# Latent attention: side steps interleaved by the engine that empties their bank, values in front of the scores, scale moved into q

## The chip, the cores and the metric

One NeuronCore of a Trainium2 chip runs the whole program. The metric is the device time of one execution in microseconds (us). TensorE is called PE in the profile, VectorE DVE, ScalarE ACT, GpSimd POOL, SyncE SP.

## What is computed

A decoder with two layers, of which this change touches one part, the cross attention of layer 1 (called latent attention here). For each of 16 batches, 100 latent rows (the running x) attend to 361 context rows and to themselves, with 16 heads of 64:

```python
xn = layer_norm(x, g_x, b_x)          # context, 361 x 256
ln = layer_norm(latents, g_l, b_l)    # 100 x 256
q = ln @ Wq                           # 256 x 1024
k, v = split(concat([xn, ln], axis=1) @ Wkv)   # 461 rows
q = q * 64 ** -0.5
sim = where(full_mask, einsum('bhid,bhjd->bhij', q, k), max_neg)
out = einsum('bhij,bhjd->bhid', softmax(sim), v) @ Wout
return layer_norm(out, g_o, b_o)      # added to x, normed again
```

## The kernel before

The program is a row of stages, one after the other, with a barrier between them: self attention, cross attention, an expert adapter, bucket attention, latent attention (`latent_attention`, tiles named `la_`), and a routed feed-forward. Only latent attention is touched. All of it is in float32 apart from the mask.

The 16 heads of a batch are handled in 8 pairs. Each engine has its own instruction queue, written out by hand, and the queues meet in counting semaphores. A batch has 8 slots (m = 0 to 7), one for each pair of heads. In slot m the queues do this:

- PE: `scores(m)` (2 mask matmuls in bfloat16 and 4 of 461 columns, into one of two pairs of PSUM banks), `turn` of the pair before (8 transposes of the probabilities), `values` of the pair before that (16 matmuls), and up to three side steps.
- DVE: `norm` of the pair before (one reciprocal, two multiplications), `maxima(m)` (one reduction over both heads, then the multiplication by minus the scale), in slots 3 to 7 some of the layer norms (`out_norm` in 3, `x_norm` in 4, `inputs` for the batch after next in 5, `apply_inputs` in 6, `mask` in 7), and then its part of the side steps.
- ACT: the first side step if it is ACT's, `exps(m)` (two Exp with their sums), the second, `evac` (copies the turned probabilities out of PSUM), `sums` (copies the values' result), the third.

The side steps prepare the next batch, and end the one before. They are named in `SLOTS`: `fl` and `fc0`, `fc1` turn the inputs, `fk0` to `fk7` project keys, `fq0`, `fq1` queries, `fv00` to `fv31` values, and `by` is the output projection of the batch before. All of them write one PSUM bank, `pf` (in the profile `la_side`): a step waits until the step before it has been read out (`above(pe, s_R, n)`). ACT reads `fl`, `fc` and `fk` out, DVE reads `fq`, `fv` and `by`. Each queue runs through the steps in the order of `SLOTS`. Before the first batch, the run-in does the steps of batch 0 alone, one after the other, and the last batch (15) has no side step but `by`.

PE's order in a slot is: scores, side step 1, turn, side step 2, values, side step 3.

Of the kernel before, what the change touches and what calls it, by code (L numbers as in the profile page):

```python
# [10 lines left out]
ALU = mybir.AluOpType  # L11
ACT = mybir.ActivationFunctionType
AX = mybir.AxisListType.X

P = 128
NB, T, D = 16, 100, 256
# [28 lines left out]
class Stage:  # L45
# [15 lines left out]
    def sb(self, name, shape, dt=F32):  # L61
        return self.ctx.enter_context(self.nc.sbuf_tensor(f"{self.name}_{name}", shape, dt))

    def ps(self, name, shape):
        return self.ctx.enter_context(self.nc.psum_tensor(f"{self.name}_{name}", shape, F32))

    def sem(self, name):
        self.sems.append(self.nc.alloc_semaphore(f"{self.name}_{name}"))
        return self.sems[-1]
# [13 lines left out]
class Side:  # L83
# [11 lines left out]
    def steps(self, i, m):  # L95

        first, last = isinstance(i, int) and i == 0, isinstance(i, int) and i == NB - 1
        keep = [s for s in self.all if not (first and s[0] == "b") and not (last and s[0] == "f")]
        if first:
            base = len(self.fronts)  # L100
        else:
            base = 2 * len(self.fronts) + (i - 1) * len(self.all)
        return [(s, base + keep.index(s)) for s in self.slots[m] if s in keep]

    def prologue(self):
        return [(s, n) for n, s in enumerate(self.fronts)]
# [661 lines left out]
def cross_attention(nc, X, ident, d):  # L768
# [4 lines left out]
    keys = [P, P, SC - 2 * P]  # L773
    SLOTS = [["fx"], ["fc0", "fq"], ["fc1", "bo"], ["bp", "fv0"], ["fk0", "by"], ["fk1", "fv1"], [], []]
    NORM = 6
    st = Stage(nc, "ca")
    with st:
# [35 lines left out]
        s_dv = sem("dve_chain")  # L813
        side = Side(SLOTS, s_F, s_R)
        NW = 5
# [612 lines left out]
def bucket_attention(nc, X, ident, d):  # L1428
# [3 lines left out]
    SCALE = D ** -0.5  # L1432
    SLOTS = [["fx", "fq"], ["fh"], [], ["fv", "bo"]]
    st = Stage(nc, "ba")
    with st:
# [33 lines left out]
        s_dv, s_dq, s_df, s_pl = sem("setup_chain"), sem("quad_chain"), sem("step_chain"), sem("pool_chain")  # L1469
        side = Side(SLOTS, s_F, s_R)  # L1470
        NW = 5 + HG
# [299 lines left out]
def latent_attention(nc, X, ident, d):  # L1771
# [3 lines left out]
    NC, SK = 4, SC + T  # L1775
    KP_ = NC * P
    MP = NH // 2
    SCALE = DX ** -0.5
    ckeys = [P, P, SC - 2 * P]
    keys = [min(P, SK - c * P) for c in range(NC)]  # L1780
    SLOTS = [["fl", "fc0", "fc1"], ["fk0", "fk1", "fk2"], ["by", "fk3", "fk4"], ["fk5", "fk6", "fk7"],
             ["fq0", "fq1", "fv00"], ["fv01", "fv10", "fv11"], ["fv20", "fv21", "fv30"], ["fv31"]]
    st = Stage(nc, "la")
    with st:
        sb, ps, sem = st.sb, st.ps, st.sem
# [11 lines left out]
        qT = [sb(f"qT{b}", [P, NE, T]) for b in range(2)]  # L1797
        nm = [sb(f"nm{b}", [T, 2]) for b in range(2)]
# [8 lines left out]
        pS = ps("pS", [P, 4, 512])  # L1807
        pPT = ps("pPT", [P, 2, 512])
        pav, pf = ps("pav", [P, 4, T]), ps("side", [P, 512])
# [3 lines left out]
        s_xs, s_F, s_R = sem("xs_staged"), sem("side_filled"), sem("side_read")  # L1813
        s_cmv, s_cln, s_crs, s_n = (sem(n) for n in ("input_stats", "input_log", "input_rstd", "inputs_normed"))
        s_mb = sem("mask_ready")
        s_S, s_mx, s_P, s_Z = sem("scores_in_psum"), sem("max_ready"), sem("exp_ready"), sem("probs_ready")
# [3 lines left out]
        s_dv, s_dn, s_dy, s_dz = sem("setup_chain"), sem("input_chain"), sem("out_chain"), sem("norm_chain")  # L1820
        side = Side(SLOTS, s_F, s_R)
        NW = 10

        with nc.Block() as block:
# [25 lines left out]
            def _(pe):  # L1850
# [36 lines left out]

                def scores(i, b, m):
                    n = i * MP + m
                    if m == 0:  # L1890
                        pe.wait_ge(s_R, side.front_done(i))
                        pe.wait_ge(s_mb, i + 1)
                    above(pe, s_P, n - 1)
                    half = [slice(DX * e, DX * (e + 1)) for e in range(2)]
                    o = [pS[0:T, 2 * (m % 2) + e, 0:SK] for e in range(2)]
                    for e in range(2):
                        nc.tensor.matmul(o[e], row0[half[e], 0:T], mb[b][half[e], 0:SK], start=True, stop=False)
                    for e in range(2):
                        last = nc.tensor.matmul(o[e], qT[b][half[e], m, :], kT[b][half[e], m, :],  # L1899
                                                start=False, stop=True)  # L1900
                    last.then_inc(s_S, 1)
# [7 lines left out]
                                                       pr[m % 2][:, e, c * P:(c + 1) * P], ident[0:T, 0:T])  # L1909
                    last.then_inc(s_PTp, 1)  # L1910

                def values(n, b, m):
                    pe.wait_ge(s_PT, n + 1)
                    above(pe, s_av, n)
                    for c in range(NC):
                        for e in range(2):
                            last = nc.tensor.matmul(pav[DX * e:DX * (e + 1), m % 4, :],  # L1917
                                                    v[b][:, c, (2 * m + e) * DX:(2 * m + e + 1) * DX],
                                                    pT[m % 2][:, e, c * T:(c + 1) * T], start=c == 0, stop=c == NC - 1)
                    last.then_inc(s_AV, 1)  # L1920

                def body(i, b):

                    first = isinstance(i, int) and i == 0
                    for m in range(MP):
                        n = i * MP + m
                        small = side.steps(i, m) + [None] * 3

                        def between(s):
                            if s and s[0] == "by":  # L1930
                                pe.wait_ge(s_av, i * MP)
                                step(*s, i - 1, b)
                            elif s:
                                step(*s, i + 1, 1 - b)
                        scores(i, b, m)
                        between(small[0])
                        if m >= 1 or not first:
                            turn(n - 1, (m - 1) % MP)
                        between(small[1])
                        if m >= 2:  # L1940
                            values(n - 2, b, m - 2)
                        elif not first:
                            values(n - 2, 1 - b, MP - 2 + m)
                        between(small[2])

                pe.wait_ge(s_w, 16 * NW)
# [3 lines left out]
                over_batches(pe, body)  # L1950
                n = NB * MP
                turn(n - 1, MP - 1)
                values(n - 2, 1, MP - 2)
                values(n - 1, 1, MP - 1)
                pe.wait_ge(s_av, n)
                for name, k in side.epilogue():
                    step(name, k, NB - 1, 0)
# [2 lines left out]
            def _(dv):  # L1960
# [35 lines left out]
                def step(name, n, i, b):  # L1996
                    if name[:2] == "fq":
                        dv.wait_ge(s_F, n + 1)
                        nc.vector.tensor_copy(qT[b][:, 4 * int(name[2]):4 * int(name[2]) + 4, :],
                                              pf[:, 0:4 * T].rearrange("p (q t) -> p q t", q=4)).then_inc(s_R, 1)  # L2000
                    elif name[:2] == "fv":
                        c, h = int(name[2]), int(name[3])
                        dv.wait_ge(s_F, n + 1)
                        nc.vector.tensor_copy(v[b][0:keys[c], c, h * 512:(h + 1) * 512], pf[0:keys[c], :])\  # L2004
                            .then_inc(s_R, 1)
                    elif name == "by":
                        dv.wait_ge(s_F, n + 1)
                        nc.vector.tensor_copy(y0[:], pf[0:T, 0:D]).then_inc(s_R, 1)
                        dv.wait_ge(s_R, n + 1)
                        link(nc.vector.bn_stats(stats[:], y0[:]), i, 1)  # L2010
                        nc.vector.memset(gap[:], 0.0)
                        nc.vector.bn_aggr(mv[:], stats[:]).then_inc(s_mv, 1)
# [21 lines left out]
                def maxima(i, m):  # L2034
                    n = i * MP + m
                    dv.wait_ge(s_S, n + 1)
                    above(dv, s_P, n - 1)
                    nc.vector.reduce_max(nm[m % 2][:], pS[0:T, 2 * (m % 2):2 * (m % 2) + 2, 0:SK], AX)\  # L2038
                        .then_inc(s_mx, 1)
                    dv.wait_ge(s_mx, 2 * n + 1)  # L2040
                    nc.vector.tensor_scalar(nm[m % 2][:], nm[m % 2][:], -SCALE, None, ALU.mult).then_inc(s_mx, 1)  # L2041

                def norm(n, m):
                    dv.wait_ge(s_P, n + 1)
# [57 lines left out]
            def _(ac):  # L2102
# [29 lines left out]

                def exps(i, m):
                    n = i * MP + m
                    ac.wait_ge(s_mx, 2 * n + 2)
                    above(ac, s_PTp, n - 1)
                    for e in range(2):
                        ins = nc.scalar.activation(pr[m % 2][:, e, 0:SK], pS[0:T, 2 * (m % 2) + e, 0:SK], ACT.Exp,  # L2138
                                                   bias=nm[m % 2][:, e:e + 1], scale=SCALE,
                                                   accum_out=zs[m % 2][:, e:e + 1])  # L2140
                    ins.then_inc(s_P, 1)

# [45 lines left out]
                n = NB * MP  # L2188
# [458 lines left out]
```

## Time and profile before

| | us |
|---|---|
| median of 3 runs | 3083.02 |
| lowest, highest | 3065.78, 3084.93 |
| profiled execution, its own time | 3084.47 |
| its span in the profile | 3082.7 |
| run-in of latent attention, batches 0 to 14, batch 15 up to its last turn | 60.51, 955.05, 33.88 |

The time of the profiled execution is the span and 1.8 us around it. A clock of 1.00 in the rows is 2.4 GHz, the other level, 0.50, is 1.2 GHz; a mean between them tells the share of the time at each. Of a PE row in a timeline, the start is the first matmul's, and several matmuls of one step are merged with their count behind the x. The last row of the table is cut from the trace at the first matmuls of the scores of batch 0 (1789.06 us) and of batch 15 (2744.11 us).

### The profile page before, as it was taken

Reading aid. Unit: us, or ns where it says so; the run is one execution under the profiler, and the core shown is the slowest. Engines: PE = TensorE matmul, PEld = TensorE weight load, DVE = VectorE, ACT = ScalarE, POOL = GpSimd, SP = SyncE. Lnnn points to the kernel's source line nnn. Section 1 sums busy time; section 2 is a strip of 40 time slices with the busy share of each in tenths; the row PEclk is TensorE's granted clock in tenths of the full one; section 3 lists DMA queues with packets and bytes.
Section 4 is the critical chain, followed back from the end, with each engine's and each line's share of the span. In section 5 each row is a group of like instructions: output and inputs, shape, how many; then the busy total and the mean of one; then the engine's idle time right before and its main releaser. Section 6 shows DMA issues by size and latency. Waiting matters only on the chain. (4 is left out here: it accounts for less than half of the span.)

```text
span 3082.7 us, 44584 instructions
## 1 busy us (share of the span) xinstructions
PE 2467.7 (80%) x15278; PEld 1459.9 (47%) x15279; DVE 1723.8 (56%) x3404; ACT 1187.7 (39%) x2418; POOL 433.1 (14%) x360
## 2 busy tenths in 40 slices
PE   3777777774999999876777489999999999994793
PEld 1333333332666666553444145554455544553572
DVE  3899999993555555534777234444544454453123
ACT  1666666663333333222444124343343433440110
POOL 1333333220111111002343000000000000001102
PEclk9888888885999999977787699999999999995897
DMA  3000000000000000200000200000000000006111
GB/s 110 1 1 0 0 0 0 0 0 27 13 13 10 14 10 10 68 4 9 0 0 0 72 5 11 5 5 5 5 10 5 5 5 5 5 1 229 40 32 51
DMA packets 50289, 60.41 MB, mean 20 GB/s; under 512 B 9764, under 2 KB 44889, under 8 KB 49770
## 3 DMA queue, kind: packets, MB, share of 16 engines
q1 hardware_dynamic: 47218, 53.69, 5.5%
q0 software_dynamic: 3008, 5.91, 0.7%
q8 instruction: 36, 0.59, 0.1%
q14 instruction: 27, 0.22, 0.0%
HBM read 51.06 MB, written 8.52 MB: 19 GB/s over the span
## 5 line engine op out<-in xcount | busy, mean ns | idle before, releaser
L1880 PE MATMUL la_side<-la_wkv,la_inT 128*128 128x512 f32 (+1 forms) x512 | 258.0, 627 | 49.2 <-DVE la_v L2004 48.3
L2138 ACT ACTIVATE la_pr<-la_pS,la_nm 100x461 f32<-100x461 f32 x256 | 163.1, 644 | 267.9 <-DVE la_nm L2041 267.9
L1868 PE MATMUL la_side<-la_inT,la_wkv 128*128 128x461 f32 x512 | 240.1, 592 | 7.6 <-ACT la_kT L2125 6.9
L2038 DVE TENSOR_REDUCE la_nm<-la_pS 100x2 f32<-100x922 f32 x128 | 142.7, 1115 | 182.9 <-PE la_pS L1899 182.9
L300 PE MATMUL sa_pS<-sa_qT,sa_kTm 128*100 128x400 f32 x512 | 195.1, 504 | 7.3 <-DVE sa_L L471 7.3
L2004 DVE COPY la_v<-la_side 128x512 f32<-128x512 f32 (+1 forms) x128 | 87.7, 685 | 180.1 <-PE la_side L1880 180.0
L895 PE MATMUL ca_pS<-ca_kT,ca_qTm 128*100 128x361 f32 x512 | 187.0, 488 | 0.5 <-DVE ca_va L974 0.5
L1075 ACT ACTIVATE ca_pr<-ca_pS,ca_nm 100x361 f32<-100x361 f32 x256 | 129.7, 559 | 125.2 <-DVE ca_nm L1009 125.1
L1006 DVE TENSOR_REDUCE ca_nm<-ca_pS 100x2 f32<-100x722 f32 x128 | 116.3, 908 | 96.6 <-PE ca_pS L895 96.5
L604 ACT ACTIVATE sa_L<-sa_L 100x800 f32<-100x800 f32 x128 | 111.3, 870 | 146.8 <-DVE sa_L L471 146.8
L1880 PEld LDWEIGHTS la_side<-la_wkv,la_inT 128*128 128x128 f32 (+1 forms) x512 | 82.3, 180 | 163.6 <-DVE la_v L2004 91.5
L2206 POOL TENSOR_TENSOR la_xb<-io_X,la_bo 100x256 f32<-100x256 f32 x16 | 11.6, 727 | 958.4 <-DVE io_X L2031 958.4
L2125 ACT COPY la_kT<-la_side 128x461 f32<-128x461 f32 x128 | 69.5, 543 | 198.8 <-PE la_side L1868 198.8
L1868 PEld LDWEIGHTS la_side<-la_inT,la_wkv 128*128 128x128 f32 x512 | 89.3, 194 | 101.9 <-issue 54.8
L479 DVE TENSOR_TENSOR sa_L<-sa_L,sa_sm 100x3200 f32<-100x3200 f32 x32 | 122.4, 3824 | 19.8 <-ACT sa_L L611 19.8
L470 DVE TENSOR_TENSOR sa_sm<-sa_pS,sa_causal 100x800 f32<-100x800 f32 x128 | 125.9, 984 | 5.4 <-PE sa_pS L300 5.3
L1908 PEld LDWEIGHTS la_pPT<-io_ident,la_pr 100*128 100x128 f32 x1024 | 100.9, 142 | 52.5 <-issue 38.2
L1917 PEld LDWEIGHTS la_pav<-la_pT,la_v 128*64 128x64 f32 x2048 | 93.6, 139 | 62.7 <-issue 56.9
L1899 PE MATMUL la_pS<-la_kT,la_qT 64*100 64x461 f32 x512 | 120.8, 550 | 0.0
L1917 PE MATMUL la_pav<-la_pT,la_v 128*64 128x100 f32 x2048 | 118.7, 259 | 0.4 <-ACT la_oT L2150 0.4
L1908 PE MATMUL la_pPT<-io_ident,la_pr 100*128 100x100 f32 x1024 | 110.1, 250 | 7.1 <-DVE la_pr L2048 7.1
L916 PE MATMUL ca_pav<-ca_pT,ca_va 128*32 128x100 f32 x1536 | 115.7, 253 | 0.0
(385 smaller groups left out, 4924.1 us busy)
## 6 DMA issues: line engine op xcount, KB each, us to landing
rf_w<-in_L_ffn_W SPq DMA_DIRECT2D x16, 1024.0 KB, 13.3
ca_cn<-in_ctx SPq DMA_DIRECT2D x16, 256.0 KB, 2.7
la_cn<-in_ctx SPq DMA_DIRECT2D x16, 256.0 KB, 2.7
rows_in<-io_zero SPq DMA_DIRECT2D x20, 128.0 KB, 4.6
rb_xr<-rows_in POOLq DMA_DIRECT2D x20, 128.0 KB, 2.2
rows_out<-rb_yr SPq DMA_DIRECT2D x20, 128.0 KB, 1.7
ea_wc<-in_L_ffn_conv_W SPq DMA_DIRECT2D x1, 2048.0 KB
la_wkv<-in_L_xattn_Wkv SPq DMA_DIRECT2D x1, 2048.0 KB
```

The source lines that it names most:

```text
L300: last = nc.tensor.matmul(pS[0:T, 2 * (m % 2) + e, 0:NBR * T], kTm[:, g, h + e, :], qT[:, g, :, :], start=True, stop=True)
L470: cm.after(nc.vector.tensor_tensor(sm[:, g, h:h + 2, :, :], two, mask, ALU.add))
L479: nc.vector.tensor_tensor(L[:, par, g].rearrange("p h r t -> p (h r t)"), L[:, par, g].rearrange("p h r t -> p (h r t)"), sm[:, g].rearran ...
L895: last = nc.tensor.matmul(pS[0:T, 2 * (m % 2) + e, 0:SC], qTm[b][:, h // HG, h % HG, :], kT[b][:, h // HG, :], start=True, stop=True)
L1075: ins = nc.scalar.activation(pr[m % 2][:, e, 0:SC], pS[0:T, 2 * (m % 2) + e, 0:SC], ACT.Exp, bias=nm[m % 2][:, e:e + 1], scale=SCALE)
L1868: last = nc.tensor.matmul(pf[:, 0:SK], wkv[:, k, e * P:(e + 1) * P], inT[:, k, :], start=k == 0, stop=k == KD - 1)
L1880: last = nc.tensor.matmul(pf[0:keys[c], :], inT[:, k, c * P:c * P + keys[c]], wkv[:, k, o:o + 512], start=k == 0, stop=k == KD - 1)
L1899: last = nc.tensor.matmul(o[e], qT[b][half[e], m, :], kT[b][half[e], m, :], start=False, stop=True)
L1908: last = nc.tensor.transpose(pPT[:, e, c * T:(c + 1) * T], pr[m % 2][:, e, c * P:(c + 1) * P], ident[0:T, 0:T])
L1917: last = nc.tensor.matmul(pav[DX * e:DX * (e + 1), m % 4, :], v[b][:, c, (2 * m + e) * DX:(2 * m + e + 1) * DX], pT[m % 2][:, e, c * T:(c ...
L2038: nc.vector.reduce_max(nm[m % 2][:], pS[0:T, 2 * (m % 2):2 * (m % 2) + 2, 0:SK], AX)\
L2138: ins = nc.scalar.activation(pr[m % 2][:, e, 0:SK], pS[0:T, 2 * (m % 2) + e, 0:SK], ACT.Exp, bias=nm[m % 2][:, e:e + 1], scale=SCALE, accu ...
```

## The change

Five edits, all in latent attention:

1. `SLOTS` is written anew, so that most neighbouring side steps are read out by different engines. The same 22 steps are done.
2. PE's order in a slot becomes: values, scores, side step 1, turn, side step 2, side step 3. The values of a pair are still taken two slots after its scores.
3. The scores no longer wait for all side steps of their batch: scores 0 and 4 wait for the keys and queries of the next four pairs, and the first values of a batch wait for the rest.
4. The scale is multiplied into q while q is read out of PSUM (a `tensor_copy` becomes a `tensor_scalar` with one multiplication), and Exp gets no scale.
5. `reduce_max` gives the negated maximum itself (`negate=True`), and the `tensor_scalar` on 100x2 elements behind it (L2041) goes, with its wait and its count of `s_mx`.

```diff
+    def later(self, a, b):
+
+        return max(a, b, key=self.all.index)
...
-    SLOTS = [["fl", "fc0", "fc1"], ["fk0", "fk1", "fk2"], ["by", "fk3", "fk4"], ["fk5", "fk6", "fk7"],
-             ["fq0", "fq1", "fv00"], ["fv01", "fv10", "fv11"], ["fv20", "fv21", "fv30"], ["fv31"]]
+    SLOTS = [["fl", "fc0", "fc1"], ["fk0", "fv00", "fk1"], ["by", "fv01"], ["fk2", "fv10", "fk3"],
+             ["fq0", "fv11", "fk4"], ["fk5", "fv20", "fq1"], ["fk6", "fv21", "fk7"], ["fv30", "fv31"]]
...
                 def scores(i, b, m):
                     n = i * MP + m
+                    if m % 4 == 0:
+                        pe.wait_ge(s_R, side.read_of(i, side.later(f"fk{m + 3}", f"fq{m // 4}")))
                     if m == 0:
-                        pe.wait_ge(s_R, side.front_done(i))
                         pe.wait_ge(s_mb, i + 1)
...
-                def values(n, b, m):
+                def values(n, i, b, m):
+                    if m == 0:
+                        pe.wait_ge(s_R, side.front_done(i))
                     pe.wait_ge(s_PT, n + 1)
...
+                        if m >= 2:
+                            values(n - 2, i, b, m - 2)
+                        elif not first:
+                            values(n - 2, i - 1, 1 - b, MP - 2 + m)
                         scores(i, b, m)
                         between(small[0])
                         if m >= 1 or not first:
                             turn(n - 1, (m - 1) % MP)
                         between(small[1])
-                        if m >= 2:
-                            values(n - 2, b, m - 2)
-                        elif not first:
-                            values(n - 2, 1 - b, MP - 2 + m)
                         between(small[2])
...
-                        nc.vector.tensor_copy(qT[b][:, 4 * int(name[2]):4 * int(name[2]) + 4, :],
-                                              pf[:, 0:4 * T].rearrange("p (q t) -> p q t", q=4)).then_inc(s_R, 1)
+                        nc.vector.tensor_scalar(qT[b][:, 4 * int(name[2]):4 * int(name[2]) + 4, :],
+                                                pf[:, 0:4 * T].rearrange("p (q t) -> p q t", q=4), SCALE, None,
+                                                ALU.mult).then_inc(s_R, 1)
...
-                    nc.vector.reduce_max(nm[m % 2][:], pS[0:T, 2 * (m % 2):2 * (m % 2) + 2, 0:SK], AX)\
+                    nc.vector.reduce_max(nm[m % 2][:], pS[0:T, 2 * (m % 2):2 * (m % 2) + 2, 0:SK], AX, negate=True)\
                         .then_inc(s_mx, 1)
-                    dv.wait_ge(s_mx, 2 * n + 1)
-                    nc.vector.tensor_scalar(nm[m % 2][:], nm[m % 2][:], -SCALE, None, ALU.mult).then_inc(s_mx, 1)
...
-                    ac.wait_ge(s_mx, 2 * n + 2)
+                    ac.wait_ge(s_mx, n + 1)
                     above(ac, s_PTp, n - 1)
                     for e in range(2):
                         ins = nc.scalar.activation(pr[m % 2][:, e, 0:SK], pS[0:T, 2 * (m % 2) + e, 0:SK], ACT.Exp,
-                                                   bias=nm[m % 2][:, e:e + 1], scale=SCALE,
+                                                   bias=nm[m % 2][:, e:e + 1],
                                                    accum_out=zs[m % 2][:, e:e + 1])
```

## Rows read from the trace of the kernel before

**Rows 1.** The page: busy time, share and instructions of each engine
```profile
PE 2467.7 (80%) x15278; PEld 1459.9 (47%) x15279; DVE 1723.8 (56%) x3404; ACT 1187.7 (39%) x2418; POOL 433.1 (14%) x360
```

**Rows 2.** Windows: batches 0 to 14, batch 15; busy time by engine, clock, DMA
```profile
1789.06:2744.11 955.05, 892.45 (x5344) 485.94 (x5344) 453.40 (x1113) 377.18 (x980) 15.00 (x28) 0.99 0.02 6
2744.11:2777.99 33.88, 26.18 (x258) 17.11 (x257) 21.48 (x54) 19.48 (x54) 0.72 (x1) 1.00 0.00 1
```

**Rows 3.** Waits of PE in batches 0 to 14: total us, times, longest
```profile
PE la_side L1880 <- DVE la_v L2004: 42.8, 28, 1.8
```

**Rows 4.** Timeline of POOL, one row per batch: start us, length, instruction, idle before
```profile
2077.24 0.73 POOL L2206 TENSOR_TENSOR la_xb<-io_X,la_bo 100x256 f32<-100x256 f32 x1 [64.18 <-DVE io_X L2031]
...
2142.41 0.73 POOL L2206 TENSOR_TENSOR la_xb<-io_X,la_bo 100x256 f32<-100x256 f32 x1 [64.10 <-DVE io_X L2031]
...
2206.04 0.73 POOL L2206 TENSOR_TENSOR la_xb<-io_X,la_bo 100x256 f32<-100x256 f32 x1 [62.56 <-DVE io_X L2031]
```

**Rows 5.** Timeline of PE in slots 3 to 5 of one batch
```profile
2067.28 1.82 PE L1868 MATMUL la_side<-la_inT,la_wkv 128*128 128x461 f32 x4
2068.93 0.85 PE L1908 MATMUL la_pPT<-io_ident,la_pr 100*128 100x100 f32 x8
2069.73 1.82 PE L1868 MATMUL la_side<-la_inT,la_wkv 128*128 128x461 f32 x4
...
2080.65 1.98 PE L1880 MATMUL la_side<-la_wkv,la_inT 128*128 128x512 f32 x4
2082.57 0.40 PE L1897 MATMUL la_pS<-la_mb,la_row 64*100 64x461 bf16 x2
...
2083.67 1.98 PE L1880 MATMUL la_side<-la_wkv,la_inT 128*128 128x512 f32 x4
...
2088.07 3.46 PE L1880 MATMUL la_side<-la_wkv,la_inT 128*128 128x512 f32 x4 [1.73 <-DVE la_v L2004]
```

**Rows 6.** Timeline of all engines, end of slot 7 and slot 0
```profile
2042.57 0.91 PE L1917 MATMUL la_pav<-la_pT,la_v 128*64 128x100 f32 x16
...
2043.40 0.40 PE L1897 MATMUL la_pS<-la_mb,la_row 64*100 64x461 bf16 x2
...
2044.71 1.12 DVE L2038 TENSOR_REDUCE la_nm<-la_pS 100x2 f32<-100x922 f32 x1 [0.39 <-PE la_pS L1899]
...
2047.48 0.65 ACT L2121 ACTIVATE la_inT<-la_side,la_bx,la_gx 128x361 f32<-128x361 f32 x1
...
2048.02 0.83 ACT L2146 COPY la_pT<-la_pPT 128x800 f32<-128x800 f32 x1
...
2048.19 0.53 PE L1862 MATMUL la_side<-io_ident,la_cn 128*128 128x128 f32 x3 [1.07 <-ACT la_inT L2121]
...
2048.65 0.40 PE L1897 MATMUL la_pS<-la_mb,la_row 64*100 64x461 bf16 x2
```

**Rows 7.** Timeline of the run-in, side steps alone on PE
```profile
1742.06 3.44 PE L1868 MATMUL la_side<-la_inT,la_wkv 128*128 128x461 f32 x4 [0.63 <-ACT la_kT L2125]
...
1767.02 1.99 PE L1880 MATMUL la_side<-la_wkv,la_inT 128*128 128x512 f32 x4 [0.67 <-DVE la_qT L1999]
...
1769.78 1.99 PE L1880 MATMUL la_side<-la_wkv,la_inT 128*128 128x512 f32 x4 [0.78 <-DVE la_v L2004]
```

**Rows 8.** Timeline of all engines, one slot of batch 15
```profile
2770.47 1.11 DVE L2038 TENSOR_REDUCE la_nm<-la_pS 100x2 f32<-100x922 f32 x1
...
2771.62 0.17 DVE L2041 TENSOR_SCALAR la_nm<-la_nm 100x2 f32<-100x2 f32 x1
2771.82 0.65 ACT L2138 ACTIVATE la_pr<-la_pS,la_nm 100x461 f32<-100x461 f32 x1 [1.47 <-DVE la_nm L2041]
...
2773.08 0.82 ACT L2146 COPY la_pT<-la_pPT 128x800 f32<-128x800 f32 x1
...
2773.78 0.26 ACT L2150 COPY la_oT<-la_pav 128x100 f32<-128x100 f32 x1
2774.16 1.11 DVE L2038 TENSOR_REDUCE la_nm<-la_pS 100x2 f32<-100x922 f32 x1
```

More of the change, by code:

```diff
@@ L1952, in _ @@
                 turn(n - 1, MP - 1)
-                values(n - 2, 1, MP - 2)
-                values(n - 1, 1, MP - 1)
+                values(n - 2, NB - 1, 1, MP - 2)
+                values(n - 1, NB - 1, 1, MP - 1)
                 pe.wait_ge(s_av, n)
```

## The prediction

> **What bounds the kernel now.** I read the page first: PE is busy 80% of the span, more than any other engine [rows 1]. That is a mean over six stages, so I cut out the one that changes. In its batches 0 to 14 PE is busy 892.5 of 955.1 us at a granted clock of 0.99, while DVE and ACT are under half busy [rows 2]. The stage is bound by PE's own work, and what can be won is only the idle time between its matmuls (about 62 us) and the time at the low clock: a mean of 0.99 is some 2% of 955 us, 20 us, at half rate, which costs at most 10. Work taken from DVE or ACT gains nothing unless PE waits for it. The waits of PE show where it does: 42.8 us in 28 waits for DVE's copy of the values, two per batch [rows 3]. The timeline puts one of them, 1.73 us, behind `fv01` in slot 5 [rows 5]; the other, of 1.35 us, is in slot 6 (2 x 14 waits of 3.1 us in sum per batch). In both slots DVE does a layer-norm block between the maximum and the copy. A third wait, 1.07 us, is ACT's: `fc1` in slot 0 waits for the copy of `fc0`, which is queued behind `exps(0)` [rows 6]. One batch takes 63.6 us, and 65.2 with a clock drop in it [rows 4]: there the matmuls behind the 1.73 us wait took 3.46 us in place of 1.98 [rows 5].
>
> In batch 15, without side steps, another thing bounds: the cycle maximum, exps, norm, next maximum, 3.69 us per slot (2770.47 to 2774.16) [rows 8], with PE often idle: 26.2 of 33.9 us [rows 2].
>
> **Part 1, the new slots: the old stalls.** With `fv` now second in its slot, the copy has the first step, the turn and the `fv` itself as cover. After the scores DVE needs about 1.3 us to the start of the maximum and 1.1 for it [rows 6], and the longest block of layer norm adds about 2 us (it ends before 4.5 us), while the `fv` ends at about 1.10 + 1.65 + 0.80 + 1.98 = 5.5 us [rows 5]. So DVE is free in time in slots 3 to 6, and both waits go: -3.1 us per batch.
>
> **Part 2, the order: new gaps.** The bank `pf` is still one. Before, each side step had something of PE's own behind it: the turn (0.80), the values (0.83), or the scores (1.10) [rows 5, 6]. The turn covers the copy of an `fk` exactly: `fk6` starts at 2069.73 as the turn ends [rows 5]. Now side steps 2 and 3 are neighbours with nothing between them, and it does not matter which engine empties the bank, since step 3 waits for it. The run-in shows this bare sequence: from one `fv` to the next 2.76 us, with 0.78 us of idle PE [rows 7], against 1.92 us from an `fv` to the scores, where nothing is waited for [rows 5]. The gap costs 0.84 us. Five slots have it (1, 3, 4, 5, 6), always behind an `fv`: +4.2 us per batch. In slot 7 the turn covers all but 0.1 us of `fv30`'s copy; slot 2 has no third step.
>
> **Part 3, slot 0.** It took 5.25 us (2043.40 to 2048.65) [rows 6]. Take the start of its scores as zero. `fc1` starts at 4.79; without L2041 the exps and all behind them come 0.2 us earlier (0.17 us of the instruction [rows 8] and its step): 4.59, and it has issued at 5.05. Then the values come, and no longer the scores. They wait for `evac` of the pair before and, since `values` also waits for the previous `sums`, for that too: `evac` starts at 4.62 - 0.2 = 4.42, `sums` starts 0.70 behind it and takes 0.26 [rows 6, 8], so the values start at 5.43 and the next scores at 6.27. Slot 0 grows by 1.0 us. The values that used to lie between `fc0` and `fc1` were cover, and are now outside.
>
> Per batch: -3.1 + 4.2 + 0.1 + 1.0 = +2.2 us. Fifteen batches have side steps for the next: +33 us. I walked the other slots in the same way: `norm` is always done over 1 us before its turn, except in slot 0 (about 0.2), and `evac` ends before `values` needs it.
>
> **Part 4, batch 15.** ACT's order is exps(m), evac(m-1), sums(m-2). The next maximum now needs the next scores, these are queued behind `values(m-1)` on PE, and these need evac and sums. From the start of the exps: sums end 2.22 us later (2771.82 to 2773.78 + 0.26) [rows 8], values at 2.27, scores at 3.10, maximum 1.31 later [rows 6] at 4.4, next exps 1.15 later at 5.5. The cycle was 3.69 us and is 5.5, though L2041 is gone: +1.8 us for seven cycles, less where `by` already lengthened one: +12 us (bounds: -1.5, if only L2041 counts, to +15).
>
> **Part 5, what is on no path.** In batches 0 to 14 the removed L2041 (128 x 0.17 us in all) lies beside PE's side steps except in slot 0, where it is counted. Nothing in the trace shows a negating reduction; bounds are the plain 1.11 us [rows 8] and that plus the removed 0.17, and I take the plain one. Also q's read-out with a multiplication has no row: its copy is covered by the turn or followed by values and scores, so between -0.1 and +0.5 us per copy come to nothing to a few us; I take 0. Of that the Trainium skill, "VectorE: DVE Perf Modes", section "Why PSUM operands drop a tier", says that float32 from PSUM runs at the plain rate, copy or not; no row here shows the multiplication from PSUM. The two waits that PE's scores and first values now have are for steps a slot or more old. The run-in does the same steps with the same gaps in another order: 0, give or take 3.
>
> **Part 6, the clock.** A drop costs about 1.5 us (65.17 - 63.63) [rows 4] and came behind a 1.73 us wait. These go: -6 us of the 10. But slot 0 now idles 1.7 us before `fc1` and 0.4 behind it, with small steps between: bounds no drop (0) and one in each batch (+22); I take half, +11. In batch 15, PE is busy only some 2.8 of 5.5 us per cycle, where it was 2.8 of 3.7 at the full clock [rows 2, 8]. At half rate values and scores, which are on the new path, take about twice their 1.9 us: bounds 0 and +13; I take +6.
>
> **Sum.** 33 + 12 - 6 + 11 + 6 = +56 us on the profiled execution's own 3084.5: 3140 us, 1.8% slower. That execution is within 2 us of the median of the runs, so this is also the forecast for the median.
>
> **The rivals.** (a) *The gap behind side step 2 is not paid*, because PE finds the bank emptied or loads weights meanwhile. For it: matmul ends are modelled and the weight loads overlap. Against it: the bare sequence in the run-in, eight times over. The time is 3140 - 75 g for a gap smaller by g; with no gap left, 3077, not slower. It decides from a gap below 0.1 us; with the clock undisturbed, below 0.3. Chance 0.10, with 0.05 for over 1% faster, where slot 0 is also shorter than I read. (b) *Only the steady part counts*: batch 15 doesn't lengthen, and the clock stays up. 3084.5 + 33 - 6 = 3111, within 1%. For it: the clock stayed at 1.00 in batch 15. Against it: the order of three queues. Chance 0.10. (c) *The clock falls with each small gap.* Five gaps per batch, each with its next step at 1.2 GHz: 3.44 us for an `fk` as against 1.82 [rows 5, 7], +1.6 x 75 = +122: 3262 us. For it: `fk` steps with 0.63 us gaps between them stayed at that level at 1742 us [rows 7]. Against it: at 1767 and 1769 us steps with gaps of 0.67 and 0.78 us ran at the full 1.99 [rows 7]. The Trainium skill, "TensorE: Matmul & The Clock Gate", section "A second HAM failure mode: psum-queue depth-cycling", says that idle bits between matmul groups that wait for PSUM can make the clock swing. By that rule (c) would happen; the run-in of this trace shows both. Chance 0.05.
>
> **How the numbers follow.** The forecast has 0.75. Some 1% is what a measurement of this kernel can tell from no change, as its runs lie 0.6% apart. Above +1% (3114) are the forecast, but for a small part, and (c): 0.79. Within 1%: (b) and half of (a) and that part: 0.16. Faster: 0.05. The range reaches down past (b), with 15 us for a run on the low side of the spread, to 3098, and up to the upper bounds of the clock terms (11 + 7), rounded to 3165; (c) and (a) stay outside.
>
> **What would show it.** In the profile after: no wait of PE for DVE above 1 us in slots 5 and 6; about 70 waits of 0.8 us, before `fk1`, `fk3`, `fk4`, `fq1`, `fk7`, all for DVE's copy of `la_v`; a batch period near 65.8 us; slot 0 of 6.3 us; exps of batch 15 5.5 us apart, with the scores' releaser before DVE's maximum; L2041 gone and the reduction at 1.1 us. A period below 63.6 us would mean that Part 2 is wrong; an even 3.5 us in batch 15, Part 4.

## The result

The changed kernel takes 3142.0 us (median of 4 runs, 3136.3 to 3145.7), the kernel before 3077.6 us beside it (4 runs, 3065.8 to 3084.9). The ratio is 1.021, with a 95% interval from 1.017 to 1.025: the change makes the kernel 2.1% slower. The profiled execution took 3145.65 us, with a span of 3143.9 us, 61.2 us more than before.

**Where the 61.2 us are.** Cutting both traces at the same four marks (first side step of the stage, first scores of batch 0, first scores of batch 15, last turn) gives:

| stretch, us | before | after | difference |
|---|---|---|---|
| all earlier stages, up to the first side step | 1728.6 | 1722.2 | -6.4 |
| run-in | 60.5 | 59.6 | -0.9 |
| batches 0 to 14 | 955.1 | 1000.5 | +45.5 |
| batch 15, to its last turn | 33.9 | 56.3 | +22.4 |
| rest | 304.7 | 305.3 | +0.6 |

The earlier stages are not touched, and the start of this stage lies between 1713.0 and 1728.6 us in the nine profiles of this study. The whole loss lies in the batches. The windows after, with the columns of [rows 2] (start and end, length, then the busy time of PE, PEld, DVE, ACT and POOL, the clock and the DMA):

```profile
1781.75:2782.29 1000.54, 905.65 (x5363) 489.77 (x5362) 433.95 (x994) 374.85 (x981) 15.13 (x28) 0.98 0.02 5
2782.29:2838.57 56.28, 37.23 (x243) 23.17 (x241) 20.67 (x46) 18.69 (x52) 0.72 (x1) 0.72 0.00 1
```

PE is busy 905.7 us in batches 0 to 14, where it was 892.5, and idle 95 us where it was 63 [rows 2]. In batch 15 the mean clock is 0.72, and it was 1.00. The waits of PE in batches 0 to 14 (total us, times, longest), where [rows 3] had 28 waits for DVE of up to 1.8 us:

```profile
PE la_side L1872 <- DVE la_v L2012: 47.0, 60, 0.8
PE la_side L1866 <- ACT la_inT L2127: 24.5, 15, 1.9
PE la_side L1878 <- DVE la_v L2012: 11.8, 15, 0.8
PE la_pav L1924 <- ACT la_oT L2156: 7.0, 15, 1.2
```

Seventy-five waits for DVE's copy of the values, none above 0.8 us, five in each of the 15 batches. A new releaser stands in the list: the values wait for ACT's `sums` (`la_oT`), 15 times. The wait for the copy of `fc0` has grown from 15.8 to 24.5 us in all. The batch period on POOL's timeline, as in [rows 4]:

```profile
2150.65 0.74 POOL L2212 TENSOR_TENSOR la_xb<-io_X,la_bo 100x256 f32<-100x256 f32 x1 [66.42 <-DVE io_X L2039]
...
2216.59 0.73 POOL L2212 TENSOR_TENSOR la_xb<-io_X,la_bo 100x256 f32<-100x256 f32 x1 [64.86 <-DVE io_X L2039]
...
2284.07 0.74 POOL L2212 TENSOR_TENSOR la_xb<-io_X,la_bo 100x256 f32<-100x256 f32 x1 [66.41 <-DVE io_X L2039]
```

The starts are 65.94 and 67.48 us apart, without and with a clock drop (a stretch at 1.2 GHz). They were 63.63 and 65.17.

The timeline of PE, a slot 0 with a clock drop first, then a gap in slot 3 and one in slot 5; it answers to [rows 5]:

```profile
2051.06 0.53 PE L1866 MATMUL la_side<-io_ident,la_cn 128*128 128x128 f32 x3 [1.70 <-ACT la_inT L2127]
2052.01 1.32 PE L1924 MATMUL la_pav<-la_pT,la_v 128*64 128x100 f32 x16 [0.42 <-ACT la_oT L2156]
2053.26 0.62 PE L1902 MATMUL la_pS<-la_mb,la_row 64*100 64x461 bf16 x2
...
2055.35 2.00 PE L1872 MATMUL la_side<-la_inT,la_wkv 128*128 128x461 f32 x4
...
2074.95 1.98 PE L1884 MATMUL la_side<-la_wkv,la_inT 128*128 128x512 f32 x4
2077.72 1.82 PE L1872 MATMUL la_side<-la_inT,la_wkv 128*128 128x461 f32 x4 [0.78 <-DVE la_v L2012]
...
2095.77 2.03 PE L1878 MATMUL la_side<-la_inT,la_wq 128*128 128x100 f32 x16 [0.79 <-DVE la_v L2012]
```

From the `fv` at 2074.95 to the next side step at 2077.72 it is 2.77 us, as in the run-in before; the row's own idle time is 0.78 us. In slot 0, PE idles 1.70 us in front of `fc1`, does 0.53 us, idles 0.42 us in front of the values, and then the clock is low: the values' 16 matmuls take 1.32 in place of 0.91 us, and the scores 1.74 in place of 0.94.

A slot 0 without a drop, all engines, answers to [rows 6]:

```profile
2181.50 0.40 PE L1902 MATMUL la_pS<-la_mb,la_row 64*100 64x461 bf16 x2
...
2182.81 1.12 DVE L2046 TENSOR_REDUCE la_nm<-la_pS 100x2 f32<-100x922 f32 x1 [0.41 <-PE la_pS L1904]
...
2183.85 0.53 PE L1866 MATMUL la_side<-io_ident,la_cn 128*128 128x128 f32 x3 [0.17 <-ACT la_inT L2121]
2184.12 0.65 ACT L2144 ACTIVATE la_pr<-la_pS,la_nm 100x461 f32<-100x461 f32 x1 [0.33 <-DVE la_nm L2046]
...
2185.38 0.65 ACT L2127 ACTIVATE la_inT<-la_side,la_bx,la_gx 128x361 f32<-128x361 f32 x1
...
2185.92 0.83 ACT L2152 COPY la_pT<-la_pPT 128x800 f32<-128x800 f32 x1
```

From the start of the scores (2181.50), the exps start at 2.62, the copy of `fc0` at 3.88 and `evac` at 4.42 us, each 0.2 us earlier than before, but PE comes to them sooner than that.

One cycle of batch 15, all engines, answers to [rows 8]:

```profile
2821.87 0.65 ACT L2144 ACTIVATE la_pr<-la_pS,la_nm 100x461 f32<-100x461 f32 x1 [4.85 <-DVE la_nm L2046]
...
2823.12 0.82 ACT L2152 COPY la_pT<-la_pPT 128x800 f32<-128x800 f32 x1
...
2823.83 0.26 ACT L2156 COPY la_oT<-la_pav 128x100 f32<-128x100 f32 x1
...
2824.23 1.60 PE L1924 MATMUL la_pav<-la_pT,la_v 128*64 128x100 f32 x16 [2.74 <-ACT la_oT L2156]
...
2825.76 0.62 PE L1902 MATMUL la_pS<-la_mb,la_row 64*100 64x461 bf16 x2
...
2827.66 1.12 DVE L2046 TENSOR_REDUCE la_nm<-la_pS 100x2 f32<-100x922 f32 x1 [3.37 <-PE la_pS L1904]
2828.82 0.65 ACT L2144 ACTIVATE la_pr<-la_pS,la_nm 100x461 f32<-100x461 f32 x1 [4.73 <-DVE la_nm L2046]
```

From exps to exps it is 6.95 us (2821.87 to 2828.82), where it was 3.69. In order: `evac`, `sums`, values behind them at the low clock (1.60 us), scores behind the values, the maximum behind the scores, the exps behind the maximum. The maximum used to start with no idle time of DVE in front of it [rows 8]; now DVE idles 3.37 us until the scores are there.

### The profile page after: what moved, and what is told of

It reads as the page before. It is cut to its first block and busy times, and to the rows that moved or that the text cites. A ratio compares the mean times of both kernels' runs of the same rounds, so it can differ in the third digit from the quotient of the medians.

```text
span 3143.9 us, 44398 instructions
## 1 busy us (share of the span) xinstructions
PE 2475.9 (79%) x15278; PEld 1462.0 (47%) x15279; DVE 1702.9 (54%) x3276; ACT 1184.6 (38%) x2418; POOL 433.6 (14%) x360
## 5 line engine op out<-in xcount | busy, mean ns | idle before, releaser
L1904 PE MATMUL la_pS<-la_kT,la_qT 64*100 64x461 f32 x512 | 132.2, 597 | 0.0
L2152 ACT COPY la_pT<-la_pPT 128x800 f32<-128x800 f32 x128 | 106.1, 829 | 32.0 <-PE la_pPT L1913 29.6
```

## The experiments

Two groups of runs, each beside the kernel before on its chip (median 3078.6 us beside e1 to e4, 3080.2 beside e5 to e7; 7 runs each).

**e1, the old order of PE's queue, all else as changed.**

```diff
-                        if m >= 2:
-                            values(n - 2, i, b, m - 2)
-                        elif not first:
-                            values(n - 2, i - 1, 1 - b, MP - 2 + m)
                         scores(i, b, m)
...
                         between(small[1])
+                        if m >= 2:
+                            values(n - 2, i, b, m - 2)
+                        elif not first:
+                            values(n - 2, i - 1, 1 - b, MP - 2 + m)
                         between(small[2])
```

> The changed kernel with the old order in PE's queue (the values between side step 2 and side step 3), all else as changed. My theory: the five gaps of 0.8 us per batch are covered again, slot 0 falls from 6.3 to about 5.05 us, batch 15 goes back to a cycle of 3.5 us; a batch takes about 60.5 us without a clock drop, and the whole about 3030 us, 1.7% faster than the kernel before. Rival (the new slots themselves cost, since each side step now goes back and forth between two busy engines): the time stays above 3100 us. Rival (mostly the clock): the drops stay at one in nearly each batch.

Measured: 3021.4 us, ratio to before 0.982 (0.980 to 0.984), so some 120 us less than the changed kernel. A batch takes 60.4 us (60.34 and 60.42 in turn), and the two windows are:

```profile
1783.95:2687.39 903.44, 885.29 (x5346) 483.30 (x5346) 432.62 (x994) 384.52 (x980) 15.07 (x28) 1.00 0.02 6
2687.39:2719.84 32.45, 26.16 (x258) 17.10 (x256) 20.11 (x46) 19.00 (x53) 0.72 (x1) 1.00 0.00 1
```

All of the loss is in the order, and the other edits are a gain of 1.8%. PE has no wait for DVE left but one of 0.8 us in all these batches, and the mean clock is 1.00, with one drop, in slot 0 of batch 0. Both rivals fall.

**e2, the kernel before with the new order alone.**

```diff
+                        if m >= 2:
+                            values(n - 2, b, m - 2)
+                        elif not first:
+                            values(n - 2, 1 - b, MP - 2 + m)
                         scores(i, b, m)
...
                         between(small[1])
-                        if m >= 2:
-                            values(n - 2, b, m - 2)
-                        elif not first:
-                            values(n - 2, 1 - b, MP - 2 + m)
                         between(small[2])
```

> The kernel before with the new order in PE's queue alone. My theory: the order is what costs. With the old slots it makes six bare neighbours (fk1 to fk2, fk3 to fk4, fk6 to fk7 at 0.63 us of idle PE; fq1 to fv00, fv10 to fv11, fv21 to fv30 at 0.7 to 0.8), slot 0 grows by 1.2 us and the two old waits for DVE in slots 5 and 6 stay: about +5.7 us per batch, +86 us, and batch 15 grows by 20 us or more; about 3195 us in all, slower than the changed kernel. Rival (the new slots cost): near 3083 us.

Measured: 3200.8 us, ratio 1.040 (1.038 to 1.043). PE's waits in batches 0 to 14:

```profile
PE la_side L1880 <- DVE la_v L2004: 54.5, 58, 1.3
PE la_side L1868 <- ACT la_kT L2125: 27.9, 44, 0.6
PE la_side L1862 <- ACT la_inT L2121: 27.8, 15, 2.1
PE la_pav L1917 <- ACT la_oT L2150: 24.4, 30, 1.6
PE la_side L1880 <- DVE la_qT L1999: 10.0, 15, 0.7
```

The order alone costs 4%, and every kind of gap is there: 44 of 0.63 us behind an `fk`, 15 of 0.67 behind `fq1`, and 58 for the copy of the values: two new ones of 0.78 us per batch, and the two old ones in 14 batches, now about 1.32 and 0.93 us long. The gaps follow from the neighbours in one bank, whichever engine reads it: `fk1` and `fk2`, both read by ACT, pay 0.63 us, and `fq1` and `fv00`, both read by DVE, 0.67. A batch takes 69.8 us, and 71.4 with a clock drop, which nearly each has. That is 6.2 us more than before, where I had expected 5.7: the values of slot 0 also wait for `sums`, 1.12 us in front of the scores, besides the 0.42 us in slot 1 (30 waits in the list). Batch 15 takes 55.1 us in place of 33.9, so the order alone lengthens it.

**e3, the kernel before with the scale in q and the negated maximum alone** (edits 4 and 5 of the diff).

> The kernel before with the scale in q and the negated maximum alone. My theory: 0.2 us per batch in slot 0 and 0.2 us per slot in batch 15, in all 4 to 5 us, 0.15%, which is at the edge of what can be measured; the cycle of batch 15 is 3.5 us as against 3.69. Rival (DVE's small instruction is on the path in every slot): 0.2 us x 128 = 26 us faster, 3057 us.

Measured: 3059.3 us, ratio 0.994 (0.992 to 0.997), 17 us faster by the ratio, and not 5. A batch takes 62.8 us as against 63.5 to 63.6, and the 65.2 of a batch with a drop is not seen. So my expectation missed, and so did its rival (26 us in every slot). Here are DVE and PE in slot 5 of e3, then DVE in slot 5 of the kernel before:

```profile
2002.06 1.11 DVE L2039 TENSOR_REDUCE la_nm<-la_pS 100x2 f32<-100x922 f32 x1
...
2003.09 1.07 DVE L1973 BATCH_NORM_STATS2 la_cst<-la_cn 128x6 f32<-128x256 f32 x3
...
2004.82 0.66 DVE L2005 COPY la_v<-la_side 128x512 f32<-128x512 f32 x1
...
2005.54 0.70 PE L1880 MATMUL la_side<-la_wkv,la_inT 128*128 128x512 f32 x1 [1.35 <-DVE la_v L2005]
```

```profile
2018.97 1.11 DVE L2038 TENSOR_REDUCE la_nm<-la_pS 100x2 f32<-100x922 f32 x1
...
2020.39 1.08 DVE L1973 BATCH_NORM_STATS2 la_cst<-la_cn 128x6 f32<-128x256 f32 x3
...
2022.13 0.66 DVE L2004 COPY la_v<-la_side 128x512 f32<-128x512 f32 x1
```

From the start of the maximum to the start of the first layer-norm instruction it is 1.03 us, and the copy of `fv01` comes 2.76 us after the maximum. In the kernel before these are 1.42 and 3.16 us: the removed instruction of 0.17 us stood in front of the copy that PE waited for. PE's waits for DVE fall from 42.8 to 34.8 us in sum. I had counted L2041 in slot 0 alone. It also lay on the path in slots 5 and 6, as long as those had their waits (here 1.35 and 1.16 us, before 1.73 and 1.35). With 0.4, 0.2 and 0.2 us in slots 5, 6 and 0 (there the wait for `fc0`, 12.8 us in sum in place of 15.8) that is 0.8 us per batch, 12 us. In the profiles batches 0 to 14 shrank by 16.9 us and batch 15 by 1.4; the rest of the 16.9 fits the clock, with one drop in these batches in place of five, but was not measured by itself.

**e4, the changed kernel with the old order in batch 15 alone.** (`take()` holds the four lines that issue the values.)

```diff
+                        late = isinstance(i, int) and i == NB - 1
+                        if not late:
+                            take()
                         scores(i, b, m)
...
                         between(small[1])
+                        if late:
+                            take()
                         between(small[2])
```

> The changed kernel with the old order in PE's queue in batch 15 alone. My theory: batch 15 goes from 56 us (first scores to last turn) back to about 32.5, and the whole from 3142 to about 3119 us; batches 0 to 14 stay at 66 us each. Rival (batch 15 is long because PE is at half clock there, whatever the order): it stays above 45 us.

Measured: 3115.7 us, ratio 1.013 (1.010 to 1.016). Batch 15:

```profile
2772.16:2805.06 32.90, 26.24 (x257) 17.11 (x257) 20.74 (x47) 18.80 (x52) 0.73 (x1) 1.00 0.01 1
```

It is 32.9 us long at the full clock, as against 56.3 at 0.72. The order made both the length and the low clock there. Batches 0 to 14 stay at 998 us.

**e5, the kernel before with the new slots alone** (edit 1 of the diff).

> The kernel before with the new slots alone (old order, scores wait for all side steps, scale and maximum as before). My theory: the waits for DVE in slots 5 and 6 go, nothing new comes: a batch takes 60.5 to 60.7 us in place of 63.6, and the whole about 3033 us, 1.6% faster than before. Rival (the new slots cost): slower than 3083 us.

Measured: 3028.3 us, ratio 0.984 (0.981 to 0.987). A batch takes 60.7 us. The new slots are worth 1.6%: PE's 28 waits for DVE in slots 5 and 6 are gone, and the run holds one clock drop in batches 0 to 14, as against five before.

**e6, the changed kernel with the values' old place in slot 0 alone.**

The edit is e4's with another condition:

```diff
-                        late = isinstance(i, int) and i == NB - 1
+                        late = m == 0
```

> The changed kernel with the old place of the values in slot 0 alone (behind side step 2; so also in slot 0 of batch 15). My theory: slot 0 falls from 6.4 to about 5.05 us, and the clock drops, which come in slot 0, become rare: 15 x 1.3 = 20 us less, and up to 14 us more by the clock, 3110 us or so against 3142. The five gaps of 0.78 us stay. Rival (the drops come from the many small gaps): about nine drops stay, and the time is no lower than 3120 us.

Measured: 3124.7 us, ratio 1.015 (1.012 to 1.018), where the rival's time was. PE's waits in batches 0 to 14:

```profile
PE la_side L1872 <- DVE la_v L2018: 47.1, 60, 0.8
PE la_side L1866 <- ACT la_inT L2133: 15.8, 15, 1.5
PE la_side L1878 <- DVE la_v L2018: 11.8, 15, 0.8
PE la_pav L1924 <- ACT la_oT L2162: 7.0, 15, 1.2
PE la_pPT L1913 <- DVE la_pr L2060: 4.1, 14, 0.3
```

The 75 gaps stay (58.9 us in sum, and 58.8 in the changed kernel), and in the profiled execution there is no clock drop in any of the 15 batches. So the small gaps alone do not bring drops; the drops of the changed kernel came with its slot 0, and the rival's reason falls, though its time was the better one. The profile is of one execution, of 3120.5 us; two of the other three took 3129 to 3130 us, and whether they had drops no trace shows. But the clean period fell only from 65.9 to 65.4 us: the wait for `fc0` is shorter, while the values of slot 1 still wait for `evac` and `sums` (7.0 us, as before), and the turn of slot 0 now waits 0.3 us for `norm`, since its cover in front of the scores is gone. I had ascribed to slot 0 alone what two neighbouring slots share. Batch 15 gains little: 53.7 us at a mean clock of 0.84, where the changed kernel had 56.3 at 0.72.

**e7, a version meant to win:** e1 with `fc1` moved on.

```diff
-    SLOTS = [["fl", "fc0", "fc1"], ["fk0", "fv00", "fk1"], ["by", "fv01"], ["fk2", "fv10", "fk3"],
+    SLOTS = [["fl", "fc0"], ["fc1", "fk0", "fv00"], ["by", "fk1", "fv01"], ["fk2", "fv10", "fk3"],
```

> A version meant to win: the changed kernel with the old order in PE's queue and with fc1 moved to slot 1 (slots fl fc0 / fc1 fk0 fv00 / by fk1 fv01 / fk2 fv10 fk3 / fq0 fv11 fk4 / fk5 fv20 fq1 / fk6 fv21 fk7 / fv30 fv31), so that the copy of fc0, which is queued behind the exps, has values and scores as cover. My theory: the last wait of 1 us per batch goes, 59.5 us per batch and about 3013 us, 2.2% faster than before. Rival (ACT's queue in slot 1, with evac, sums, fc1 and fk0 in a row, gives the wait back): no faster than e1.

Measured: 3005.6 us, ratio 0.977 (0.974 to 0.979). PE's waits in batches 0 to 14 are 4.5 us in all:

```profile
PE la_side L1866 <- ACT la_inT L2121: 3.2, 15, 0.9
PE la_side L1884 <- ACT la_kT L2131: 0.6, 1, 0.6
PE la_side L1866 <- ACT la_inT L2127: 0.4, 1, 0.4
PE la_pPT L1913 <- ACT la_pT L2152: 0.3, 1, 0.3
```

A batch takes 59.58 us, and PE is busy 59.2 to 59.3 us of it; the one wait left in such a batch is 0.2 us. It beats both kernels: 2.3% faster than before, 4.3% faster than the changed one.

## Why the prediction was right

The forecast was 3140 us, the measured time is 3142.0. That the two are 2 us apart is in part luck. In the profiles latent attention lost 67.0 us (45.5 and 22.4, less 0.9 in the run-in), where the sum had 56; the earlier stages, which the change does not touch, happened to be 6.4 us shorter, and the median lies 3.7 us below the profiled execution. What holds beyond the luck are the terms, one by one, on the profiled executions:

| step | forecast, us | measured, us |
|---|---|---|
| Part 1, old waits | -3.1 per batch | no wait for DVE above 0.8; e5: batch 63.6 to 60.7 |
| Part 2, gaps | 5 of 0.84 per batch | 75 of 0.78 idle, 2.77 from step to step |
| Part 3, slot 0, scores to scores | 5.25 + 1.0 = 6.27 | 6.37 (2181.50 to 2187.87) without a drop |
| batch without a drop | 63.6 + 2.2 = 65.8 | 65.9 |
| Parts 4 and 6, batch 15 | +12, +6 by the clock | +22.4 |
| Part 5, q's read-out with the multiplication, the negated maximum | 0 | 0.575 as before; 1.118, was 1.115 |
| Part 6, clock in batches 0 to 14 | -6 + 11 = +5, at 1.5 each about 3 drops more | 10 drops, was 5 |
| batches 0 to 14 in all | +33 + 5 = +38 | +45.5 |
| sum | +56 | +67.0 in latent attention, +61.2 in the whole span |

*Part 1 and Part 2* are shown by undoing: without the order (e1, e5) all five gaps go, with the order alone (e2) there are gaps at each of its own neighbours. *Part 3* had the times right, each within 0.1 us (`fc0`'s copy at 3.88, `evac` at 4.42). *Part 4* had the chain right: at the full clock the cycle from values to values was 5.6 us (2804.39 to 2809.97), as against 5.5 forecast; most of the other cycles took about 7 us, with the values and scores at the low clock.

*What was mis-sized.* The clock, both times too low. In batch 15 half of its upper bound of 13 us was taken (6 us); with 12 us for the chain, some 10 of the 22.4 us are left for the clock, an estimate by difference. In batches 0 to 14 there were five drops more in place of about three. e4 shows that in batch 15 neither the length nor the low clock remains with the old order. And one sentence of Part 5, that L2041 is on the path only in slot 0: e3 shows it in slots 5 and 6 too in the kernel before. That did not enter the sum, because in the changed kernel these slots have lost their waits by Part 1. The range was also not quite what its working gives (3111 less 15 is 3096, and 3140 with 18 is 3158, where 3098 and 3165 stand); the measured time lies inside either.

*The rivals.* (a), the unpaid gap, is refuted by the 75 waits of 0.78 us. (b), only the steady part, is refuted by batch 15's +22.4 us and ten drops. (c), the clock falling with each small gap, is refuted by the changed kernel itself, with 75 gaps, ten drops and 1.82 us for the `fk` behind a gap (2077.72), and by e6: 75 gaps, no drop. The Trainium skill ("TensorE: Matmul & The Clock Gate", section "A second HAM failure mode: psum-queue depth-cycling") says of another kernel that short idle times of TensorE between matmul groups, as they go through the PSUM banks, came often enough to make the clock swing. The traces here agree only where the waits are long: the clock fell in slot 0 behind 1.70 us of idle PE, a short step and 0.42 us more, and in batch 15 with 2.7 us waits. Even then it fell in only 9 of the batches 1 to 14, whose waits for `fc0` were all 1.46 to 1.91 us long; what decides between them is open.

## What to carry to other kernels

Side work that shares one PSUM bank needs something of PE's own between each two of its steps, long enough for the read-out (here 0.55 to 0.69 us of copy); which engine reads it out matters only for that engine's queue. No run here gave the side steps a second bank, so what that would bring is not shown. Taking a block out of such a place turns cover into a gap, and the block itself brings its own waits along to where it is put: here the values carried `evac` and `sums` in front of the scores, the start of the longest chain. When several edits come together, undo each alone: the order cost 4%, the slots brought 1.6%, the two small ones 0.6%. These do not simply add: without the order the others together bring 1.8% (e1), since the slots and the removed instruction take from the same waits. With `fc1` moved as well it is 2.3% (e7).

## What had not been expected of the hardware

A VectorE instruction of 0.17 us in front of a layer-norm block put that off by 0.39 us (1.42 as against 1.03 us from the start of the maximum) and made PE's wait in slot 6 0.19 us longer. Without it the block's first instruction starts 0.08 us before the reduction's end; with it, 0.28 us after the small one's start. The clock stayed at 2.4 GHz through 75 waits of 0.78 us (e6) and through 28 waits of 1.06 to 1.35 us (e3, whose one drop in these batches came before them, in slot 0 of batch 0). It fell behind the wait of 1.73 to 1.75 us in slot 5 in four batches of the kernel before, and not in the others. Negating in the reduction costs nothing that shows (1.118 as against 1.115 us), and reading 128x400 out of PSUM takes 0.575 us with or without the multiplication. Of e1's lead over e5 (60.4 as against 60.7 us per batch) 0.2 us is the wait for `fc0` without L2041 (12.8 as against 16.0 us in 15 waits); the remaining 0.1 us was not taken apart, and edit 3, the later waits of scores and values, was in no run by itself.
